# A convolution's loads in longer runs and earlier, its sign tables built a stage earlier, and layer norms of two fewer instructions, in a two-block vision model on one core

## The reference, cut to what matters

```python
x = x + channel_attention(_ln_c(x), gamma)      # a 64x64 mix for each image
t = t + moe(_ln_t(t), ...)                      # 16 experts, the best 2 of them for each token
x = x + conv3x3(_ln_c(x), where(kernel >= 0, 1, -1))
t = t + graph_moe(_ln_t(t), ..., edge_index)    # attention over 262144 edges, 4 experts

def _ln_c(v, eps=1e-06):      # _ln_t is the same with 1e-05
    m = jnp.mean(v, axis=-1, keepdims=True)
    s = jnp.var(v, axis=-1, keepdims=True)
    return (v - m) / jnp.sqrt(s + eps)
```

## Time and profile before

| what | value |
|---|---|
| median of 3 runs | 1567.05 us (1566.7 to 1567.78) |
| the profiled execution, its own time | 1570.05 us |
| its span in the trace | 1568.3 us |
| DVE busy | 1131.9 us (72%) |
| POOL busy | 879.8 us (56%) |
| PE busy, its weight loads | 861.6 us (55%), 681.8 us (43%) |
| ACT busy | 451.5 us (29%) |

### The profile page before, as it was taken

The page is one execution under the profiler, slowest core; times in us unless marked ns, Lnnn a source line. Parts: engine busy times, 40 slices in busy tenths (PEclk is TensorE's granted clock), DMA queues, the critical chain, the costliest instruction groups (busy, mean ns, idle before and its releaser), DMA issues.

```text
span 1568.3 us, 36915 instructions
## 1 busy us (share of the span) xinstructions
PE 861.6 (55%) x13344; PEld 681.8 (43%) x13361; DVE 1131.9 (72%) x2794; ACT 451.5 (29%) x813; POOL 879.8 (56%) x891
## 2 busy tenths in 40 slices
PE   0322332238888881564399985666666546644430
PEld 0222322227776771554233333555555435543330
DVE  6999889876666663798866655666666556688878
ACT  0232232224444443574133330222212112122110
POOL 0045566546666662000377777777777777777740
PEclk9955555556667665776599995555555555555555
DMA  7000000022222214400311011111111111111101
GB/s 167 9 21 21 25 28 27 25 58 51 49 51 49 48 52 50 102 2 28 37 11 10 10 10 10 12 12 12 12 12 14 12 12 12 12 11 24 24 8 27
DMA packets 113952, 45.80 MB, mean 29 GB/s; under 512 B 92631, under 2 KB 108799, under 8 KB 113538
## 3 DMA queue, kind: packets, MB, share of 16 engines
q1 hardware_dynamic: 84098, 22.43, 7.5%
q0 software_dynamic: 27632, 19.12, 7.1%
q10 hardware_dynamic: 2064, 2.10, 0.7%
HBM read 28.17 MB, written 15.93 MB: 28 GB/s over the span
## 4 chain that ended last, share of the span: by engine, by line
POOL 36%; issue 12%; DVE 3%; DMA 1%; POOLq 0%; DVEq 0%; PE 0%; ACT 0%
POOL edges_rows L336 35%; DVE all_stack L2195 1%; DMA table<-edges_rows 1%; DVE all_stack L2197 0%; DMA edges_rows<-table,edges_src 0%; POOLq L76 0%; DVE all_x_sb L2198 0%; DVE all_x_sb L2199 0%; DVE edges_work L1900 0%; PE edges_acc L2441 0%; DVE edges_rows L1892 0%; DVE edges_work L1896 0%; DVE edges_as_sb L1903 0%; DVE all_ad_sb L1903 0%; POOL edges_krow L336 0%
## 5 line engine op out<-in xcount | busy, mean ns | idle before, releaser
L336 POOL DMA_INDIRECT edges_rows<-table,edges_src x576 | 564.6, 980 | 175.6 <-issue 175.6
L192 DVE TENSOR_TENSOR sorting_keys<-sorting_keys 128x512 f32<-128x512 f32 (+2 forms) x370 | 209.9, 609 | 16.8 <-ACT sorting_keys L317 13.4
L723 POOL DMA_INDIRECT x_rows<-mixture_sent,mixture_slot x128 | 144.5, 1129 | 126.8 <-DVE mixture_slot L785 88.3
L728 POOL DMA_INDIRECT y_rows<-mixture_yt,mixture_xin x144 | 157.3, 1093 | 102.5 <-ACT mixture_yt L950 78.6
L2508 ACT ACTIVATE edges_hotT<-edges_h 128x1024 bf16<-128x1024 bf16 x72 | 69.8, 1021 | 308.2 <-PE edges_h L2403 308.2
L1063 PE MATMUL mixture_bank<-mixture_xT,sorting_w_part 128*128 128x128 bf16 x864 | 109.8, 255 | 31.1 <-ACT mixture_xT L936 16.3
L1063 PEld LDWEIGHTS mixture_bank<-mixture_xT,sorting_w_part 128*128 x864 | 85.4, 105 | 56.9 <-issue 44.8
L2460 PE MATMUL edges_acc<-edges_term_parts,edges_work 128*128 128x20 bf16 x1728 | 51.6, 179 | 101.9 <-DVE edges_term_parts L1824 101.9
L2460 PEld LDWEIGHTS edges_acc<-edges_term_parts,edges_work 128*128 128x128 bf16 x1728 | 49.0, 104 | 109.4 <-issue 109.4
L2441 PE MATMUL edges_acc<-edges_end_parts,edges_work 128*128 128x4 bf16 x1728 | 51.1, 166 | 51.1 <-DVE edges_end_parts L1824 51.1
L870 DVE TENSOR_TENSOR mixture_hidden<-mixture_gated,mixture_bank 128x256 f32<-128x256 f32 x72 | 30.2, 419 | 66.0 <-PE mixture_turned L1072 31.6
(11 more groups left out here) (477 smaller groups left out, 2199.1 us busy)
## 6 DMA issues: line engine op xcount, KB each, us to landing
edges_rows<-table,edges_src POOLq DMA_INDIRECT x576, 2.4
mixture_xin<-x_rows SPq DMA_DIRECT2D x144, 49.0 KB, 1.8
all_eo<-y_rows SPq DMA_DIRECT2D x16, 256.0 KB, 3.9
y_rows<-mixture_yt,mixture_xin POOLq DMA_INDIRECT x144, 2.6
sorting_w<-in_L_ffn_w_dram SPq DMA_DIRECT2D x4, 512.0 KB, 8.3
x_rows<-mixture_sent,mixture_slot POOLq DMA_INDIRECT x128, 2.3
out_dram<-all_x_sb SPq DMA_DIRECT2D x8, 256.0 KB
constants_src_i<-in_L_ffn_edge_index_dram SPq DMA_DIRECT2D x1, 1024.0 KB, 4.9
```

Source lines behind the costliest of these rows:

```text
L192: self.st.mark(dve.tensor_tensor(target[half], source[0], source[1], (ALU.min, ALU.max)[half]))
L336: pool.indirect_dma_start(to, None, rows, where).then_inc(done, 16)
L723: pool.indirect_dma_start(x_rows, bass.IndirectOffsetOnAxis(ap=slot[g % 2][:, c, t:t + 1], axis=0), now[c][:, t, :], None).then_inc(scatte ...
L728: pool.indirect_dma_start(y_rows, bass.IndirectOffsetOnAxis(ap=xin[j % XB][:, ROWX - 2:ROWX - 1].bitcast(U32), axis=0), yt[j % YB][:, :], ...
```

## The change

**Norms.** `center` no longer scales the sums: the subtraction becomes a scalar_tensor_tensor, (sums, broadcast, times -1/64) plus image. The variance's sum goes to ACT as it is, and the root's ACTIVATE scales it by 1/64 and adds eps, as a bias of one value for each partition from a small tile `eps` that is filled in *constants*.

**Rows of results.** POOL's `iota` numbers the output rows so that for each image and partition the 8 tokens and their two choices are 16 neighbouring rows of `y_rows`, 4 KB. One load brings an image instead of two.

**Moved to mixture.** A new class `Ahead` loads the convolution's weights on SP after the experts' weights, builds the signs on DVE in the last stage of the sort, and issues the loads of images 0 and 1 on SP at mixture's end. SP waits for the landing of the scatters before that; POOL no longer does. The weights and signs lie in memory that only graph used so far (`sums`), and the results of images 0 and 1 in the tails of the two `stacks`.

**Lanes' last keys.** They are no longer loaded from DRAM. DVE copies them out of the sorted keys at mixture's end, spreads them over 128 columns after the first two images, and PE transposes that between the first two convolutions; `find_lanes` reads the result in PSUM. `starts.load` keeps the load of the rest alone, and it and `last_weights.load` now come after image 3's load.

```diff
@@ Norm
         st.link(dve.tensor_reduce(self.mean[:, :], x, X, ALU.add))
-        st.link(dve.tensor_scalar(self.mean[:, :], self.mean[:, :], -1.0 / w, None, ALU.mult))
-        st.link(dve.tensor_tensor(y, x, per_channel(self.mean[:, :], w), ALU.add))
+        st.link(dve.scalar_tensor_tensor(y, per_channel(self.mean[:, :], w), -1.0 / w, x, ALU.mult, ALU.add))
         st.link(dve.tensor_tensor(self.squares[:, :, :], y, y, ALU.mult))
-        st.link(dve.tensor_reduce(self.var[:, :], self.squares[:, :, :], X, ALU.add))
-        dve.tensor_scalar(self.var[:, :], self.var[:, :], 1.0 / w, self.eps, ALU.mult, ALU.add)\
-            .then_inc(self.var_ready, 1)
+        dve.tensor_reduce(self.var[:, :], self.squares[:, :, :], X, ALU.add).then_inc(self.var_ready, 1)
...
-        act.activation(self.root[:, :], self.var[:, :], ACT.Sqrt).then_inc(self.root_ready, 1)
+        act.activation(self.root[:, :], self.var[:, :], ACT.Sqrt, bias=self.eps, scale=1.0 / self.width).then_inc(self.root_ready, 1)
@@ mixture
             weights.load(sp)
+            ahead.load_kernel(sp)
...
             sp.wait_ge(keys_stored, 48)
+            for n in range(XB):
+                sp.wait_ge(y_sent[n], 16 * len(range(n, NTILES, XB)))
+            ahead.load_outs(sp, y_rows, 0)
+            ahead.load_outs(sp, y_rows, 1)
...
-                    pool.iota(now[c][:, :, ROWX - 2].bitcast(I32), pattern=[[P, TB]], base=c * N + g * TB * P,
-                              channel_multiplier=1).then_inc(fields, 1)
+                    pool.iota(now[c][:, :, ROWX - 2].bitcast(I32), pattern=[[2, TB]], base=g * 2 * TB * P + c,
+                              channel_multiplier=2 * TB).then_inc(fields, 1)
...
-            for n in range(XB):
-                pool.wait_ge(y_sent[n], 16 * len(range(n, NTILES, XB)))
...
                     dve.sem_inc(sort.rest_sorted, 1)
+                    ahead.take_signs(dve, ident)
...
             dve.sem_inc(sort.wanted, 1)
+            ahead.take_tops(dve, sort.keys[0])
@@ Ahead
+    def load_kernel(self, sp):
+        for half in range(2):
+            sp.dma_start(self.cw[half * C:(half + 1) * C, :].rearrange("c (a d) -> c a d", d=C),
+                         self.kernel_w.rearrange("a b c d -> c (a b) d")).then_inc(self.kernel_in, 16)
+    def load_outs(self, sp, y_rows, b):
+        rows = y_rows[b * 2 * TB * P:(b + 1) * 2 * TB * P, :].rearrange("(p r) c -> p (r c)", p=P)
+        sp.dma_start(self.outs(b), rows).then_inc(self.outs_in[b], 16)
+    def take_tops(self, dve, keys):
+        dve.tensor_copy(self.lane_top[:, :], keys[:, SC - 1:SC])
@@ Starts
+    def widen_tops(self, dve, lane_top):
+        dve.tensor_copy(self.tops[:, :], lane_top[:, :].to_broadcast([P, P])).then_inc(self.tops_wide, 1)
+    def turn_tops(self, pe, bank, ident):
+        pe.wait_ge(self.tops_wide, 1)
+        pe.transpose(bank[:, 0:P], self.tops[:, :], ident[:, :]).then_inc(self.tops_turned, 1)
     def load(self, dma):
-        with self.nc.allow_non_contiguous_dma(reason="a value per lane"):
-            tops = self.keys_dram[0:ES].rearrange("(l c) -> c l", c=SC)[SC - 1, :]
-            dma.dma_start(self.tops[:, :], tops.partition_broadcast(P)).then_inc(self.tops_in, 16)
         dma.dma_start(self.rest[:, 0:SC], self.rest_dram.rearrange("(p c) -> p c", p=P)).then_inc(self.rest_in, 16)
@@ convolve, sync
-            for half in range(2):
-                sp.dma_start(cw[half * C:(half + 1) * C, :].rearrange("c (a d) -> c a d", d=C),
-                             kernel_w.rearrange("a b c d -> c (a b) d")).then_inc(loaded, 16)
-            for b in range(B):
-                for c in range(2):
-                    rows = y_rows[c * N + b * TB * P:c * N + (b + 1) * TB * P, :].rearrange("(t p) c -> p t c", p=P)
-                    sp.dma_start(landing[:, b * TB:(b + 1) * TB, c, :], rows).then_inc(outs_in[b], 16)
-                if b == 1:
+            for b in range(2, B):
+                ahead.load_outs(sp, y_rows, b)
+                if b == 3:
                     starts.load(sp)
                     last_weights.load(sp)
```

More of the change, by code:

```diff
@@ L78, in wait_apart, with constants @@
     engine.wait_ge(sem, register)
[L81 removed]
+def constants(nc, edge_index, ident, upper, eps, p_sign, keys, x, x_sb, x_in):
     with ExitStack() as ctx:
@@ L543, in subtract_middle, with mixture @@
             .then_inc(self.subtracted, 1)
-def mixture(nc, gamma, gate_w, gate_b, x_sb, x_in, ident, upper, sort, weights, x_rows, y_rows, keys, rest):
+def mixture(nc, gamma, gate_w, gate_b, x_sb, x_in, ident, upper, eps, sort, weights, x_rows, y_rows, keys, rest, ahead):
     K, H, ws, u3 = weights.K, weights.H, weights.ws, weights.u3
@@ L1281, in split, with convolve @@
             split_weights(dve, st, w[:, :], self.left[:, 0:w.shape[1]], [parts[0][:, :], parts[1][:, :]], parts[2][:, :])
-def convolve(nc, kernel_w, x_sb, stacks, ident, starts, last_weights, landing, y_rows, spent):
+def convolve(nc, x_sb, stacks, ident, eps, starts, last_weights, ahead, y_rows, spent):
     S = 32
@@ L1366, in add_outs @@
             def add_outs(b):
-                dve.wait_ge(outs_in[b], 32)
+                dve.wait_ge(outs_in[b], 16)
+                outs = ahead.outs(b).rearrange("p (t c d) -> p t c d", t=TB, c=2)
                 for c in range(2):
-                    added.link(dve.tensor_tensor(image(b), image(b), landing[:, b * TB:(b + 1) * TB, c, :], ALU.add))
+                    added.link(dve.tensor_tensor(image(b), image(b), outs[:, :, c, :], ALU.add))
             def center2(b):
@@ L1414, in _ @@
                 low2(b)
+            starts.widen_tops(dve, ahead.lane_top)
             for b in range(B):
@@ L1669, in graph @@
         shares = [take(TP) for _ in range(2)]
-        norm = Norm(a, "norm", TP, F, 1e-5, take(TP, F))
+        norm = Norm(a, "norm", TP, F, eps[:, 1:2], take(TP, F))
         carved = 0
```

85 lines of the change are left out of this document (52 added, 33 removed).

## The result

The changed kernel takes 1540.97 us (median of 4 runs, 1539.38 to 1543.47), the one before in the same runs 1566.88: a ratio of 0.9836 (95% interval 0.9821 to 0.9852), 25.9 us faster. Forecast were 1541.5 us and 25.5. Its profiled execution took 1543.47 us with a span of 1541.6, 2.5 above its median, as that of before was 3.0 above.

A forecast was written before the change was run, and what follows sets the result against it. DVE was taken to bound routing and convolution, POOL the experts' end and, by its gathers, the edges. Savings 6.3 + 6.5 + 8.75 + 0.33 + 3.0 + 0.33 + 0.33 = 25.5 us gave median 1541.5 us, range 1534.5 to 1550.

The forecast's parts named there:

- Routing, 6.3 us: Routing stage: 16 norms on DVE's path each lose 0.40 us, saving 6.3 us (5.4 to 6.4).
- Border, 6.5: Start of the convolution: earlier drain and loads move the first add from 607.00 to 600.5, 6.5 us (5.1 to 7.7).
- The hole, 8.75: Convolution, DVE's 11.52 us wait for image 2: 8.75 us gained, two norms included, then the first convolution is late.
- the first convolution: Convolution of image 0 on PE: ends at 24.85 us after the first add, so DVE, ready at 21.35, waits 3.5.
- The norms of the convolution, 3.66: Rest of the convolution: 0.33 for image 0's second norm, 3.0 for the following iterations, 0.33 for the last norm.
- the 0.3 us taken off: Convolution loop: ACT's padding and PE's convolving (12.4 us) lag a little behind DVE's period (12.3), costing 0.3 us.
- The graph stage, 0.33: Edges, paced by POOL's 576 gathers: only the last norm, after the last gather, gains, 0.33 us.
- The root's bias, 0.07: Norms' Sqrt on ACT: a [128,1] bias adds 0.07 us where the root is waited for; the Trainium skill says about 0.093.
- PE at its lower clock: Rival, convolution: clock 0.5 throughout makes each convolution 8.3 us, losing 13 us, 1554.5 us; chance 0.05.
- its upper clock: Rival, convolution: PE at 2.4 GHz throughout, 4.2 us per convolution, removes waits, 1534.5 us; chance 0.08.
- The gathers did not slow down: Rival, edges: moved tiles slow POOL's gathers from 0.980 to 1.093 us, losing 65 us, 1606.5 us; chance 0.03.
- The signs were hidden: Forecast: hidden in the sort's 2.88 us wait. Rival: signs uncovered (2.3), drain, subtraction, loop, 7 us, 1548.5; chance 0.17.

The follow-up runs named there:

- number 2: Changed kernel with the variance's instruction back on DVE and the root without bias and scale, mean still folded: 1546.89 us, 5.4 us slower than the changed kernel.
- Numbers 4: Changed kernel with the convolution weights' load and the signs back at the convolution's start, images' early loads kept: 1546.25 us, 4.7 us slower than the changed kernel.
- 6: Changed kernel with the loads of images 0 and 1 back at the convolution's start, signs kept early: 1544.54 us, 3.0 us slower than number 5.
- 7: Changed kernel with both moves undone (weights' load and signs, loads of images 0 and 1): 1546.75 us, 5.2 us slower than number 5.
- number 1: Changed kernel with all norms in their old form (mean and variance scaled on DVE): 1553.86 us, 12.3 us slower than the changed kernel's second run.
- number 5: Changed kernel run unchanged a second time, on another chip: 1541.53 us, 27.3 us faster than the kernel before, ratio 0.9827.
- numbers 3: Kernel before with one line changed, the graph stage's loads issued behind the last image's loads: 1561.29 us, 6.5 us faster than before, ratio 0.9958.
- 9: Kernel before with only the new norms and their eps tile: 1555.88 us, 12.3 us faster than before, ratio 0.9924.

## Why the prediction was right, and where it was off

**Routing, 6.3 us: right.** The trace has 5.96 to the last scatter; over the kernels the token rows' last scatter starts 5.8 to 7.5 us earlier with the new norms. Per norm it was 0.40 as summed: 0.20 for each of the two instructions by number 2.

**Border, 6.5: right, with its parts.** The trace has 6.19. The drain was fixed work after the last scatter, as taken (3.8). The landing took 3.8 us, taken 3.5, and the issue came 1.2 us behind the last scatter, as forecast. Numbers 4, 6 and 7 show what the prediction did not say: it counted nothing for the signs here, but without their move the early loads bring the first add only 1.0 us nearer to the stage's first instruction, not 5.6.

**The hole, 8.75: right in mechanism, 0.8 too small.** The step to image 1's end was right to 0.01 us. The term that was mis-sized is the first convolution. The prediction took it from the earlier trace rows, 6.25 us; it took 5.47 here, and from 4.83 us (number 1) to 6.25 in the runs, with the same 144 matmuls. The granted clock over it was 0.67 in the earlier trace rows, 0.78 here and 0.89 in number 1, all between the levels of 1.2 GHz (0.5) and 2.4 GHz; a fixed duration for it was the error, and what sets its clock was not tried. What DVE waited is 2.89 us, not 3.5.

**The norms of the convolution, 3.66: right.** The trace has 3.24, number 5 has 4.3. The period fell to 12.23 at first, 0.81 for two norms. But the loop of ACT and PE did lag. In the profiled execution the four periods are 12.23, 12.26, 12.47 and 13.34, in number 5 12.23, 12.26, 12.53 and 12.26, so the 0.3 us taken off fits number 5 and was 1.1 too small for the other. There two convolutions in a row took 6.81 and 7.06 us, at a clock of 0.60 and 0.58, where number 5 had 6.87 and 5.55; ACT's padding came late, and with it the root that DVE waits for. The fourth period:

```profile
655.92 0.68 DVE L1415 TENSOR_TENSOR all_x_sb<-all_x_sb,convolve_conv 128x512 f32<-128x512 f32 x1
...
660.94 0.20 DVE L370 RECIPROCAL convolve_n_rstd<-convolve_n_root 128x8 f32<-128x8 f32 x1 [0.62 <-ACT convolve_n_root L382]
...
669.26 0.68 DVE L1415 TENSOR_TENSOR all_x_sb<-all_x_sb,convolve_conv 128x512 f32<-128x512 f32 x1
```

In the tail DVE waited longer, as forecast, for the same turns, 3.7 us where it was 3.2:

```profile
DVE convolve_most L1283 <- PE convolve_turns_ps L1275: 3.7, 1, 3.7
```

**The graph stage, 0.33: too small, the step that failed.** The norm after the last gather gave 0.32, as counted. The prediction counted nothing for the three norms beside the gathers, because POOL sets the pace there. The last 96 gathers are about 1 us shorter with the new norms in every trace. In the profiled pair that does not show in the whole stretch (740.25 and 740.22 us), where other gathers took longer; the 1.7 us there are the 0.32 and, for the most part, the earlier landing of the last gather (1.18), which the forecast had no term for and whose cause is open. In the sum it was hidden: the profiled execution gained 26.6 us, the forecast was 25.5.

**The root's bias, 0.07: 0.09.** The rows of the root before and after (minimum, median, maximum in ns):

```profile
L383 ACT ACTIVATE convolve_n_root<-convolve_n_var x16: 208/208/220, 611.8 to 740.8; 128x8 f32<-128x8 f32 x16
```

```profile
L382 ACT ACTIVATE convolve_n_root<-convolve_n_var,all_eps x16: 300/300/338, 599.2 to 715.8; 128x8 f32<-128x8 f32 x16
```

A difference of 0.092 us; the root got a scale of 1/64 as a constant in the same edit. The Trainium skill (ScalarE: Activation LUTs, "What ACT_TABLE_LOAD costs") gives about 0.093 for a pointer operand; the trace agrees with it, and the rows from two different lines that the prediction preferred were the worse guide. It costs only where DVE has nothing else to do: image 1's end moved by 0.65, about 2 x (0.41 - 0.09), while the period fell by the full 0.81.

**The rivals.** PE at its lower clock did not set the convolution, beyond the one period above, nor did its upper clock hold: the eight convolutions kept PE busy for 48.2 us, 50.4 before. The gathers did not slow down. The signs were hidden (1.18 us of the wait was left), the drain was unchanged but counted from an earlier point, the subtraction took 0.69. Of the time's prediction, then, each large term was right by itself. Two gained 0.8 and 1.3 us more than forecast, the three others 0.3 to 0.4 less each; that the median came within 0.5 us is in part luck.

## What to carry to other kernels

A point that several moved things must reach together is won only when all have moved: list the gates and undo one at a time, and then both: undoing one of two cost 4.7 or 3.0 us, undoing both 5.2. Ask of a hole in a load queue which transfer stands in front; one line of order gave most of what the larger rewrite gave there (8.45 of 9.56 us in that stretch). After a change that fills a wait, read the waits that are left: filling two of them with work that stood elsewhere gave 4.8 us more.

## What the runs showed of the hardware

- The load behind the broadcast of 4-byte values took 19.0 to 20.0 us to issue (before, numbers 3 and 9), wherever the pair stood, and 0.42 to 1.10 us without the broadcast ahead of it.
- The drain of POOL behind the result scatters took 3.8 us after their landing (before), and ended 3.8 us after the last of them where it was reached while they still ran, with or without another drain 144 scatters earlier; after the token rows' scatters one ended 2.0 us behind.
- POOL's gathers lengthen with a few more small DVE instructions beside them: 96 of them took 101.3 us instead of 100.3 with four such instructions more, most of it in four gathers of 1.11 to 1.17 us instead of 0.94.
- The same convolution of 144 matmuls took from 4.83 us (granted clock 0.89) to 6.25 (0.67) in different runs, which moves the point at which DVE resumes by up to 1.4 us.
